# Decays made two groups ahead in a chunked selective scan

## The reference

```python
delta = jax.nn.softplus(delta @ dt_proj_w.T + dt_proj_b)
A = -jnp.exp(A_log)
def step(h, inp):
    dt, b, xt, c = inp
    dA = jnp.exp(dt[:, :, None] * A)
    h = dA * h + dt[:, :, None] * b[:, None, :] * xt[:, :, None]
    y = jnp.einsum('bdn,bn->bd', h, c)
    return (h, y)
_, ys = jax.lax.scan(step, h0, xs)
...
return (y + x * D_param) @ out_proj_w.T
```

## Time and profile before

| | us |
|---|---|
| median of 3 runs | 1280.37 (1279.55 to 1282.02) |
| profiled execution, its own time | 1277.38 |
| its span, first to last instruction | 1276.0 |
| busy in the span: TensorE, VectorE, ScalarE, GpSimd | 1099.6, 783.6, 513.7, 325.0 |
| first and last scan start | 43.7, 656.3 |

### The profile page before, as it was taken

One profiled execution on the slowest core, in us unless ns is written; L12 is line 12 of the kernel. 1 busy time (PEld: TensorE's weight loads), 2 busy tenths in 40 slices (PEclk: granted clock), 3 DMA queues, 4 the chain that ended last, 5 costly groups with the idle time before them and its releaser, 6 DMA issues.

```text
span 1276.0 us, 30137 instructions
## 1 busy us (share of the span) xinstructions
PE 1099.6 (86%) x12251; PEld 725.4 (57%) x12331; DVE 783.6 (61%) x926; ACT 513.7 (40%) x1328; POOL 325.0 (25%) x943
## 2 busy tenths in 40 slices
PE   2588787888888788777878999999999898999998
PEld 1445454555545455444444877777887455475565
DVE  6599999999999999999972111211111656342111
ACT  3566676676767667656541111111111111212110
POOL 5144444244335434343242111111111200000000
PEclk9999999999999999999997999999999898999999
DMA  5485856444254443534235622222200300000000
GB/s 175 63 187 104 208 122 158 93 74 119 42 139 92 90 91 56 117 65 73 36 107 193 259 101 100 99 91 83 82 16 21 129 1 1 1 17 1 16 17 17
DMA packets 182203, 110.24 MB, mean 86 GB/s; under 512 B 92285, under 2 KB 176640, under 8 KB 179712
## 3 DMA queue, kind: packets, MB, share of 16 engines
q1 hardware_dynamic: 176544, 98.19, 31.3%
q0 software_dynamic: 3456, 8.48, 2.0%
q10 hardware_dynamic: 2064, 1.64, 0.5%
HBM read 63.38 MB, written 43.90 MB: 84 GB/s over the span
## 4 chain that ended last, share of the span: by engine, by line
PE 59%; DVE 16%; issue 11%; ACT 8%; DMA 2%; POOL 2%; SPq 2%; DVEq 0%; POOLq 0%; ACTq 0%
DVE h L1226 12%; PE psum L1541 11%; PE psum L1529 11%; PE psum L2043 9%; ACT decay L1058 5%; PE psum L2054 4%; PE psum L922 4%; PE psum L908 4%; PE psum L889 3%; PE psum L875 2%; PE psum L1986 2%; PE psum L1978 1%; PE psum L2030 1%; PE psum L955 1%; POOL disp_d L1456 1%
## 5 line engine op out<-in xcount | busy, mean ns | idle before, releaser
L1226 DVE TENSOR_TENSOR_SCAN h<-decay,psum 128x1024 f32<-128x1024 f32 x256 | 569.8, 2271 | 31.8 <-ACT psum L1068 21.4
L1058 ACT ACTIVATE decay<-psum 128x512 f32<-128x512 f32 x512 | 278.7, 599 | 142.8 <-PE psum L889 141.1
L908 PE MATMUL psum<-xdiag,bstat 128*128 128x64 bf16 x4096 | 167.1, 195 | 34.6 <-DVE h L1226 32.9
L908 PEld LDWEIGHTS psum<-xdiag,bstat 128*128 128x128 bf16 x4096 | 136.5, 99 | 54.0 <-DVE h L1226 43.2
L889 PEld LDWEIGHTS psum<-rows,shared 32*128 32x128 bf16 x4096 | 76.2, 94 | 142.6 <-ACT decay L1058 72.0
L1541 PE MATMUL psum<-shared,hid 128*128 128x256 f32 x640 | 139.5, 379 | 0.6 <-ACT hid L1582 0.6
L1529 PE MATMUL psum<-xdt,shared 128*128 128x320 f32 x512 | 139.2, 432 | 0.8 <-ACT xdt L1588 0.8
L922 PE MATMUL psum<-h,cstat 128*32 128x512 f32 x1024 | 138.0, 613 | 1.7 <-DVE h L1226 1.7
L1541 PEld LDWEIGHTS psum<-shared,hid 128*128 128x128 f32 x640 | 121.0, 190 | 17.2 <-issue 1.1
L1385 POOL TENSOR_TENSOR carry<-decay,h 128x16 f32<-128x16 f32 x240 | 58.3, 243 | 272.5 <-ACT decay L1058 271.1
L889 PE MATMUL psum<-rows,shared 32*128 32x64 bf16 x4096 | 106.8, 191 | 24.2 <-DMA rows<-parts_d 15.5
(11 more groups left out here) (241 smaller groups left out, 1166.6 us busy)
## 6 DMA issues: line engine op xcount, KB each, us to landing
shared<-in_w SPq DMA_DIRECT2D x16, 1024.0 KB, 4.8
xdiag<-x_parts_d SPq DMA_DIRECT2D x124, 96.0 KB
x_parts_d<-x_parts SPq DMA_DIRECT2D x16, 384.0 KB, 3.5
rows<-parts_d SPq DMA_DIRECT2D x128, 48.0 KB
x_parts_d<-x_parts SPq DMA_DIRECT2D x21, 256.0 KB, 3.3
disp_d<-r_xl SPq DMA_DIRECT2D x4, 1305.0 KB, 8.3
xd<-disp_d SPq DMA_DIRECT2D x8, 652.5 KB, 6.3
picked_d<-r_xl SPq DMA_DIRECT2D x4, 1024.0 KB, 5.2
```

The source lines that it names most:

```text
L908: ins = pe.q.matmul(to.rearrange("p d (s e) -> p s d e", e=2), bstat[:, c % 2, b, :], xdiag[:, c % 2, b, :, d, :], start=True, stop=True)
L1058: act.q.activation(decay[:, gi % NB, 8 * half:8 * half + 8, :], per_d(bank_a[half]), ACT.Exp).then_inc(sem("exp"), 1)
L1226: dve.q.tensor_tensor_scan(out=h[:, half_slot(c, half), ch:ch + G, :].rearrange("p d t -> p (d t)"), data0=decay[:, gi % NB, :, :].rearran ...
```

## The change

Three things are done:

1. TensorE: `stream(gi)` makes the inputs of gi first and directly behind them the decays of gi + 2, ahead of the group's other products. At the start the decays of groups 0 and 1 are made.
2. ScalarE: `stream(gi)` copies the carry of gi - 1 first and then takes the exponentials of gi + 1.
3. The unread products read `astat` (the table of A) as both operands. A new function, `with_unread`, counts as many for each group as before; where `bank_z` is in use in the group they stay in `decays`, and where it isn't, an event `awake` at the end of the group makes them in `bank_z`.

```diff
-def unread_after(schedule):
+def with_unread(schedule):
...
+    need = [max(0, 3 - w) if n < TOTAL - 2 else 0 for n, w in enumerate(work)]
+    unread = [(n, 0) if b else (0, n) for n, b in zip(need, busy)]
+    placed = []
+    for event in schedule[:stop]:
+        if event[0] == "stream":
+            if event[1] and unread[event[1] - 1][1]:
+                placed.append(("awake", event[1] - 1, closed[event[1] - 1]))
+        placed.append(event)
+    return placed + schedule[stop:], unread
...
                 if gi >= 2:
-                    stay_awake((gi - 1) // GROUPS, unread[gi - 2])
+                    stay_awake(unread[gi - 2][0], bank_a[1])
...
                     decays(0)
-                if gi + 1 < TOTAL:
-                    decays(gi + 1)
+                    decays(1)
                 pe.wait_ge(sem(f"tokens_ld{c % 2}"), TOKENS_LD * (c // 2 + 1))
...
                 ins.then_inc(sem("inputs"), 1)
+                if gi + 2 < TOTAL:
+                    decays(gi + 2)
...
+                elif kind == "awake":
+                    gi, z = x
+                    pe.wait_ge(sem("z_free"), z)
+                    stay_awake(unread[gi][1], bank_z)
...
             def stream(gi):
+                if gi:
+                    hand_on(gi - 1)
+                else:
+                    exps(0)
+                if gi + 1 < TOTAL:
+                    exps(gi + 1)
+
+            def exps(gi):
                 for half in range(2):
-                    e = 2 * gi + half
                     act.wait_ge(sem("prod"), gi + 1)
                     if gi >= NB:
                         act.wait_ge(sem("scan"), gi - NB + 1)
                     act.q.activation(decay[:, gi % NB, 8 * half:8 * half + 8, :], per_d(bank_a[half]), ACT.Exp
                                      ).then_inc(sem("exp"), 1)
-                if gi:
-                    hand_on(gi - 1)
```

## The result

| us | before | after |
|---|---|---|
| median of the runs | 1279.96 (1278.14 to 1282.02, 4 runs) | 1261.23 (1258.10 to 1265.15, 4 runs) |
| profiled execution, its own time | 1277.38 | 1262.25 |
| its span | 1276.0 | 1260.9 |

The change makes the kernel faster: the ratio is 0.9855, with a 95% interval of 0.9822 to 0.9887, so 14.5 to 22.8 us. A second comparison gave 0.9863 (0.9824 to 0.9902).

What follows compares the result with a forecast made beforehand. VectorE, busy with its scans, was taken as the bound, with only its idle time to win. 9.6 + 0.4 + 0.6 + 1.1 + 0.8 = 12.5 us off 1277.38 gave 1264.9, 1268 as median; range 1262.5 to 1279.

Steps and rivals of the forecast that it cites:

- (1): Turnings: inputs ahead of decays, carry copied before exponentials; 0.73 us less from turning's end to scan; with (2) 9.6 us.
- (6): End of the stage: the last turning's chain starts some 2.5 us sooner; 0.8 us taken, between 0 and 2.5.
- Rival E: Half clock: the new order moves TensorE's idle time; twelve more stretches at 1.16 us would make 1282; chance 0.03.
- (2): Turnings: unread products stand elsewhere, so y comes 0.44 us sooner; with (1) 9.6 us (from 3 to 14).
- rival D: TensorE stands in order before decays while its products wait behind; slower, 1296 or 1284 us; chance 0.05.
- (3): ScalarE's table loads before a carry's copy: only the earlier start counts, 0.4 us over both (0 to 1.7).
- (5): The seven other waits for the carry's copy, 3.31 us: a third goes, 1.1 us (0 to 3.3).
- (4): First chunk: of 3.65 us of waits at the stage's start, 0.6 us goes (from -1 to 3).
- (7): Unread products: as many as before, with other operands and sometimes another bank: 0 us.
- B: TensorE takes over as the bound: 6.6 us given back, gain 5.9, time 1274.5 us; chance 0.22.
- C: VectorE's waits only move, since totals and not order set them: time stays at 1280 us; chance 0.08.
- tail and start in full: Case of more gain than forecast, at the stage's end and start: 1263 us, chance 0.02.

Runs made afterwards that it cites:

- e1: Kernel before, with three unread products on TensorE ahead of the last tile's turning, where it idled: 0.9968 of the time before, tail 20.69 us.
- e15: Changed kernel, with GpSimd's first step of the last tile's skip input computed four times over: 0.9907 of the time before, tail 23.37 us.
- e2: Kernel before, with the last tile's skip input ahead of most scatters on GpSimd: 0.9954 of the time before, tail 17.12 us.
- e4: Changed kernel, with all unread products back in the decays: 0.9871 of the time before.
- e3: Kernel before, with ScalarE's new order alone and TensorE's decays where they were: 1.0199 of the time before.
- e6: Changed kernel, with the decays of gi + 2 kept back behind the group's y product: 0.9981 of the time before.
- e10: Changed kernel, with ScalarE's exponentials behind the copy of a chunk's first input in the group that has it: 1.0030 of the time before.
- e13: Changed kernel, with the decays of gi + 2 directly ahead of the inputs of gi: 1.0511 of the time before.
- e11: Changed kernel, with later normalized product, last skip input ahead of the scatters, and exponentials behind a chunk's first-input copy: 1.0041 of the time before.

## Why the prediction was right in direction and wrong in size

The miss is 1268.0 - 1261.2 = 6.8 us. The sum gave 12.5 us against 15.1 between the two profiled executions: 2.6. The other 4 or so come from the step from execution to median: I added the 3.0 us by which before's median stood over its profiled execution, and after's stood 1.0 below. No term of the sum is wrong there; single executions scatter. The stage's start alone lies between 43.41 and 47.23 us in the traces here, whose kernels do nearly the same up to there, and the range should have held that. The range was also narrower than the sum it came from: the upper bounds of (1) to (6) add up to 24.5 us, which is 1256, and I gave what lies below 1262.5 next to no chance.

That the sum missed by only 2.6 us is in good part luck: the tail gave 4.8 us more than I took, the turnings 4.0 less. The step that failed is the tail.

**(6), the tail, is the term that was mis-sized.** I took 0.8 us between 0 and 2.5; it was 5.6. With 5.6 in its place and all else as it stood, the forecast would have been 1263.2, inside the range. My upper bound, the earlier skip input, came in nearly full: 8.10 - 5.76 = 2.3 us. The scatters start at 644.42, 6.2 us before the last scan's end, as forecast. I gave it 0.8 because of the 4.66 us wait of ScalarE's copy, which e1 shows to be no bound there. The other 3.3 us, which e1 measures alone and e15 takes away again, lay outside my bounds: I had put the clock of the tail at nothing, without a reason. With its 3.59 us of idle time TensorE did the turning and all that followed at half clock; with that time filled (e1) or gone (e2) it did them at full clock. The row for it stood in the earlier trace rows already: four products in 1.09 us, where the same four take 0.56 at full clock. I read the releaser and not the length. Rival E knew the clock only as a loss. The Trainium skill (TensorE: Matmul & The Clock Gate, What's actually happening) says that half rate is the default and activity lifts it; e1 and e15 agree: 1.00 with most of the pause filled, and 0.98 between 656 and 659 us and 0.50 behind the pause left idle.

**(1) and (2), the turnings.** Right in mechanism, 9.6 us forecast, 5.6 found: the twelve waits of 14.28 us have 8.71 in their places in after. Ten of them fell from 10.72 to 3.82 us, 0.38 each where I took 0.25; what remains has, at the one that I followed (302.80), the cause that rival D named: exponentials late by 0.54 us in front of y. The other two, held by DMAs of y_sb in both kernels, grew from 3.56 to 4.89 (1.55 and 3.34), where I counted on a decline to about 2. The small lateness that I expected behind a turning came too, 0.25 us for GpSimd's memset in ten places, but on top of the first wait and not in its place: 2.5 us. My own signs said as much: the carry waits sum to 15.6 us where I wrote 6 to 10, and the last scan started at 648.3, not near 645.

**(3) to (5).** (3) gave nothing: the waits of 0.80 and 1.65 us are now 0.70 and 2.03. ScalarE's work up to the carry's copy is the same, as forecast, but the earlier start didn't come, since the exponentials ahead of the table loads waited 0.81 us for their decays. (4) The start gave 0.29 us less than nothing, and the five waits for inputs behind the first (2.25 us) became one of 0.54, while the carry waits of 1.40 became 1.26: 1.85 better against 0.6 taken, inside its bounds. (5) The seven other waits of 3.31 us became four of 2.87, a gain of 0.4 and not 1.1. The 2.79 us of busy time, for which I had no term, about cancel the 2.5 of the memset. So the stage gave 8.24 where (1) to (5) had 11.7. The unchanged stage took 614.85, 616.95 and 617.77 us in three traces, after's 606.61, 606.09 and 608.19, so the mean difference is 9.6; the single pair shown understates it by 1.3 us.

**(7)** is not contradicted: e4 moves the unread products back, and no cost or gain can be told.

**The rivals.** B and C did not come. E came once: the stage of after has six stretches at half clock and not five, and behind one of them (224.0 to 230.4 us) stands a scan wait of 1.61 us, which is in (5). D is the interesting one. In after TensorE does wait for exponentials at the decays, 31.2 us in 52 places, but before it waited 67.9 at the unread products, and most of the new ones cost no scan, as VectorE's shorter idle time says. How near D was, e3, e6, e10 and e13 show: one step moved on one engine costs 15 us (e6), 22 (e10) and 83 (e13) against after, and 26 (e3) against before. My argument against D (the exponentials are asked for a group sooner too) was right only because both halves came together; e3 has one half and is slower than either kernel. I gave 0.02 to a time below the forecast's own range, by tail and start in full; the tail came in full and more, the start did not.

## What to carry to other kernels

Read the length of a row beside its releaser: a product that takes twice its usual time behind a pause tells that the pause costs more than itself, and what shortens the pause earns both. Moving a producer earlier and its consumer earlier is one edit: the consumer's half alone makes an in-order engine stand still in front of its other work. Look for the ring that an order closes and add up its steps, with the groups that carry the most other work; against a bound of 2.19 us, 2.26 is already slower. And where a term has a bound of its own, let the range reach as far as the bounds do together.

## What the runs showed of the hardware that was not expected

TensorE's clock fell to 0.50 behind a pause of 1.58 us that followed a busy stretch of 1.05 and a pause of 1.18 (e15), and stayed at 1.00 behind a pause of 1.01 us with unread products in front of it (e1). But behind a pause of 3.54 us it was at 1.00 for another microsecond (e3), and behind one of 2.08 us for two (e6), so a pause's length alone tells neither whether nor when it falls. The fall in before cost 3.3 us, as the difference to e1 has it. The time up to the first scan varied by 3.8 us between executions, more than most terms of the sum, and the time behind the last slots by 5.9. ScalarE's wait at the copy of the last y, for something that the profile doesn't name, was 1.28 and 0.35 us in two executions of after, 4.66 in before and 3.25 in e11.
